# Second attention's score product moved between the halves of its query projection, and two small vector steps reordered

## The reference, cut to what matters

```python
x = _layernorm(x + _L0_attn_ref(x, qkv_weights))
# second attention
qh = _xpos(x @ Wq);  kh = _xpos(ctx @ Wk, inverse_scale=True);  vh = ctx @ Wv
scores = jnp.einsum('bld,bmd->blm', qh, kh) * decay_mask
x = _layernorm(x + scores @ vh)
x = _layernorm(x + _L0_ffn_ref(x, ...))        # shared expert, 2 of 8 routed experts
```

## Time and profile before

| what | value |
|---|---|
| median of 3 runs | 727.16 us (726.34 to 728.71) |
| profiled execution, its own time | 723.76 us |
| its span | 721.7 us |
| TensorE busy | 683.2 us, 95% |
| VectorE busy | 489.2 us, 68% |
| ScalarE busy | 478.9 us, 66% |
| GpSimd busy | 343.1 us, 48% |
| mean granted TensorE clock | 0.990 of full speed |

### The profile page before, as it was taken

One profiled execution on the slowest core, in us unless ns is written; L12 is line 12 of the kernel. 1 busy time (PEld: TensorE's weight loads), 2 busy tenths in 40 slices (PEclk: granted clock), 3 DMA queues, 4 the chain that ended last, 5 costly groups with the idle time before them and its releaser, 6 DMA issues.

```text
span 721.7 us, 21540 instructions
## 1 busy us (share of the span) xinstructions
PE 683.2 (95%) x6174; PEld 588.5 (82%) x6175; DVE 489.2 (68%) x1563; ACT 478.9 (66%) x1319; POOL 343.1 (48%) x469
## 2 busy tenths in 40 slices
PE   7989999999999999999998899889999999999994
PEld 5868888888888888888887555779999999998653
DVE  3666878888888888888896376445555555554266
ACT  0367888888888888888884242356666666666256
POOL 1001323435645455454455355055665556556495
PEclk9999999999999999999999899999999999999998
DMA  8743367424523233232336024686777777777597
GB/s 306 236 146 114 116 204 240 137 88 147 158 88 96 67 91 105 86 107 83 104 97 198 31 89 143 198 221 126 140 134 139 133 139 136 135 137 130 124 349 261
DMA packets 93947, 104.30 MB, mean 145 GB/s; under 512 B 13200, under 2 KB 86672, under 8 KB 92976
## 3 DMA queue, kind: packets, MB, share of 16 engines
q1 hardware_dynamic: 78480, 79.43, 37.2%
q0 software_dynamic: 14688, 23.26, 16.4%
q10 hardware_dynamic: 704, 0.66, 0.3%
HBM read 62.21 MB, written 41.10 MB: 143 GB/s over the span
## 4 chain that ended last, share of the span: by engine, by line
PE 78%; DVE 5%; DMA 5%; POOL 4%; issue 4%; SPq 3%; ACT 1%; DVEq 0%; POOLq 0%; ACTq 0%
PE ps L1051 15%; PE ps L1060 8%; PE ps L806 6%; PE ps L908 5%; PE ps L794 5%; PE ps L816 4%; PE ps L771 4%; PE ps L739 4%; PE ps L911 4%; PE ps L774 4%; PE ps L932 4%; DMA xg<-sent 3%; POOL first_use L715 2%; PE ps L1038 2%; PE ps L826 2%
## 5 line engine op out<-in xcount | busy, mean ns | idle before, releaser
L1118 ACT ACTIVATE prob<-ps,nmax 128x128 f32<-128x128 f32 x512 | 147.0, 380 | 27.4 <-DVE nmax L1332 27.4
L1051 PEld LDWEIGHTS ps<-xgT,attn_only 128*128 128x128 f32 x1136 | 136.0, 192 | 7.4 <-DVE ghT L1614 2.2
L1051 PE MATMUL ps<-xgT,attn_only 128*128 128x128 f32 x1136 | 138.9, 275 | 1.1 <-ACT xgT L1230 1.1
L674 POOL DMA_INDIRECT total<-rot,result_row x71 | 111.6, 1572 | 36.8 <-issue 34.3
L1332 DVE TENSOR_REDUCE nmax<-ps 128x4 f32<-128x512 f32 x128 | 82.2, 685 | 17.7 <-PE ps L794 17.0
L1614 DVE SCALAR_TENSOR_TENSOR ghT<-ps,attn_only 128x128 f32<-128x128 f32 x142 | 43.3, 347 | 71.0 <-PE ps L1051 59.3
L615 POOL TENSOR_TENSOR rot<-products 128x128 f32<-128x128 f32 x128 | 61.3, 499 | 57.1 <-DVE products L1342 57.0
L1125 ACT COPY pT<-ps 128x512 f32<-128x512 f32 x124 | 74.4, 600 | 20.8 <-PE ps L806 16.4
L806 PE MATMUL ps<-tf,prob 128*128 128x128 f32 x512 | 77.9, 275 | 4.4 <-DVE pT L1447 3.3
L641 POOL DMA_INDIRECT sent<-packets,pos x64 | 63.6, 993 | 35.6 <-PE ps L794 20.9
L1060 PE MATMUL ps<-first_use,ghT 128*128 x284 | 74.9, 386 | 0.0
(11 more groups left out here) (143 smaller groups left out, 1408.1 us busy)
## 6 DMA issues: line engine op xcount, KB each, us to landing
xg<-sent SPq DMA_DIRECT2D x71, 130.5 KB, 2.1
attn_only<-in_L_ffn_rb SPq DMA_DIRECT2D x71, 130.0 KB
first_use<-total SPq DMA_DIRECT2D x12, 512.0 KB, 8.7
total<-zeros POOLq DMA_DIRECT2D x3, 1408.0 KB, 8.0
k_dram<-first_use SPq DMA_DIRECT2D x4, 1024.0 KB, 4.6
attn_only<-in_x_turned SPq DMA_DIRECT2D x32, 128.0 KB, 2.5
attn_only<-k_dram SPq DMA_DIRECT2D x256, 16.0 KB
attn_only<-in_x SPq DMA_DIRECT2D x32, 128.0 KB, 2.7
```

Source lines behind the costliest of these rows:

```text
L674: eng.indirect_dma_start(totals[slot % 2], bass.IndirectOffsetOnAxis(ap=result_row[:, slot:slot + 1], axis=0), yw[:, slot, :], None, compu ...
L1051: mm = eng.matmul(ps[:, 2 * r + half, f * P:(f + 1) * P], w_now[:, r, c, cols:cols + P], xgT[:, r, c, :], start=(c == 0), stop=(c == DC - 1))
L1118: ins = eng.activation(prob[:, t % 2, 4 * u + n, :], SCORE[u][:, n * P:(n + 1) * P], ACT.Exp, bias=nmax[:, t % 2, 4 * u + n:4 * u + n + 1])
```

## The change

TensorE's four matmuls of the second attention's queries (two halves of two) no longer stand together ahead of the scores: the first half comes first, then the scores of the batch before, then the second half, which raises `xq_made`. VectorE takes the decay (`scx`) ahead of the products of the queries. At the end of VectorE's step the addition of the constant to the second variance stands ahead of the last mask. No instruction is added or removed.

```diff
+            def cross_queries(t, m):
+                for c in range(DC):
+                    mm = eng.matmul(Q_TURNED[:, m, :], xwq_sb[:, c, m * P:(m + 1) * P], x1T[:, t % 2, c, :],
+                                    start=(c == 0), stop=(c == DC - 1))
+                return mm
+
+            def cross_scores(t, n):
+                eng.wait_ge(rot_k_set, 2 * t + 2)
+                eng.wait_ge(rot_q_set, 2 * t + 2)
+                if live(n - 3):
+                    eng.wait_ge(pk_set, 2 * (n - 3) + 2)
+                else:
+                    bank7_read(n)
+                for m in range(2):
+                    mm = eng.matmul(SCX, rot[:, t % 2, m, :], rot[:, t % 2, 2 + m, :], start=(m == 0), stop=(m == 1))
+                mm.then_inc(scx_made, 1)
...
-                    for m in range(2):
-                        for c in range(DC):
-                            mm = eng.matmul(Q_TURNED[:, m, :], xwq_sb[:, c, m * P:(m + 1) * P], x1T[:, t % 2, c, :],
-                                            start=(c == 0), stop=(c == DC - 1))
-                    mm.then_inc(xq_made, 1)
...
+                    cross_queries(t, 0)
+                if live(n - 4):
+                    cross_scores(n - 4, n)
+                if live(t):
+                    cross_queries(t, 1).then_inc(xq_made, 1)
                 shared_between(n)
...
-                if live(t3):
-                    turned(t3, 2, Q_TURNED, xq_made, pq_set, rot_q_set)
                 if live(t4):
                     eng.wait_ge(scx_made, t4 + 1)
                     eng.tensor_tensor(scx[:, r4, :], SCX, decay, ALU.mult).then_inc(scx_set, 1)
+                if live(t3):
+                    turned(t3, 2, Q_TURNED, xq_made, pq_set, rot_q_set)
...
                     aggregate(t4, bn2, mv2, bn2_set, mv2_set)
+                    add_eps(t4, mv2, mv2_set)
                 if live(n) and live(n + 1) and n > 0:
                     lay_mask(n + 1, 3)
-                if live(t4):
-                    add_eps(t4, mv2, mv2_set)
```

More of the change, by code:

```diff
@@ L929, in step @@
                         eng.wait_ge(res2_set, n - 4)
-                    for m in range(2):
-                        for c in range(DC):
-                            mm = eng.matmul(Q_TURNED[:, m, :], xwq_sb[:, c, m * P:(m + 1) * P], x1T[:, t % 2, c, :],
-                                            start=(c == 0), stop=(c == DC - 1))
-                    mm.then_inc(xq_made, 1)
-                t = n - 4
-                if live(t):
[L938 to L946, removed]
+                    cross_queries(t, 0)
+                if live(n - 4):
+                    cross_scores(n - 4, n)
+                if live(t):
+                    cross_queries(t, 1).then_inc(xq_made, 1)
                 shared_between(n)
```

## The result

The changed kernel took 742.15 us (741.09 to 744.67, six runs), against 727.41 (724.37 to 729.93, six runs) for the kernel before: 1.0196 times as long, with a 95% interval of 1.0166 to 1.0225. The forecast was 742.9. The profiled execution took 741.09, its span 739.1, against 723.76 and 721.7.

What follows compares the result with a forecast made beforehand. TensorE was taken as the bound, with one 0.39 us stop per step. 29 x 0.50 = 14.5, plus 0.44 (step 33) and 0.8 (step 34), together 15.7, on the median 727.16 gave 742.9 us; range 735 to 748.

Steps and rivals of the forecast that it cites:

- The scores' wait: TensorE: scores behind the first query half wait for the keys' products, start at 0.78; TensorE stands for 0.33 us.
- Restarting: TensorE after a stop: scores take 0.07 us more, the output product L973 0.10 more.
- What is late next: Queries' products on VectorE end at 2.69; the output product waits until 2.84, 0.40 us later than before.
- The path through `res2`: Second path to the next projection: first residual takes 0.41, `res2` ends at 3.99, seen at 4.13, inside the projection's 4.17.
- The rival with a blocked residual: GpSimd still blocks VectorE's first residual, which takes 0.70: 0.59 us per step, 745.5 us; chance 0.13.
- The third edit: Second variance's constant ahead of the last mask on VectorE: the mask's delay is covered, earlier rows win nothing: 0.
- Per step: Projection of the next batch starts at 4.17 against 3.67: 0.50 us more per step, 29 steps, 14.5 us.
- The last steps: Pipeline's end: step 33 costs 0.44 us; step 34, with TensorE at half clock, 0.8, between 0 and 0.86.
- The sum: Steps 4 to 32 with steps 33 and 34: together 15.7 us slower, 742.9 us on the median.
- Both waits covered: Rival: keys' products end by 0.29, so scores and output lose nothing; 728.4 to 731.3 us; chance 0.09.
- The stop simply goes: Rival: output does not wait for the queries' products; 28 to 29 stops of 0.39 go, about 716 to 717 us; faster 0.07.
- The clock: Rival: TensorE's extra stops bring one more half-clock stretch, about 3 us: 746 us; chance 0.05.

Runs made afterwards that it cites:

- Experiment 4: Changed kernel with the keys' products ahead of `rden` on VectorE; 741.86 us, ratio 1.0173 to the kernel before.
- experiment 3: Kernel before with only the scores moved between the query halves on TensorE, VectorE's order unchanged; 755.05 us, ratio 1.037.
- experiment 2: Kernel before with only the decay moved ahead of the queries' products on VectorE, TensorE's list unchanged; 734.83 us, ratio 1.0078.
- experiment 8: Changed kernel with three of four query matmuls ahead of the scores instead of two; 736.63 us, ratio 1.0125 to the kernel before.
- experiment 6: Kernel before with the transposed rows put into bank 5, so they no longer wait for the decay; 724.64 us, ratio 0.9966.
- experiment 1: Kernel before with only the second variance's constant added ahead of the last mask; 727.23 us, ratio 0.9981.
- experiment 5: Kernel before with the decay placed between the two products of the queries on VectorE; 725.21 us, ratio 0.9963.
- Experiment 7: As experiment 6, with GpSimd's additions of the queries' products also waiting for the decay; 724.21 us, ratio 0.995 to the kernel before.

## Why the prediction was right, step by step

- **The scores' wait.** Put at 0.78, measured 0.77. Experiment 4 moved the keys' end and with it everything behind; experiment 3 shows that the scores' move alone makes the wait. The sentence that nothing on VectorE can give the wait back was too strong: in experiment 4 the keys' products ahead of `rden` ended 0.08 earlier, and the step was 0.09 shorter.
- **Restarting.** The scores took 0.68 and L978 0.67 after their stops, against 0.61 and 0.60; I had 0.07 and 0.10 in the sum. The interval from L978 to the projection is 1.31, not 1.33, and this is the 0.02 by which the step was put too long.
- **What is late next.** The products were put at 1.93 to 2.69 and L978 at 2.84; measured 1.94 to 2.70, and 2.84. Experiments 2 and 8 change this wait from two sides, and the step follows within 0.01 of what was expected.
- **The path through `res2`.** The statistics ended by 3.49 and `res2` at 3.97, against 3.99 forecast; the projection at 4.15 stays just behind it. With 0.42 for the residual the cover held. The rival with a blocked residual didn't come about, because GpSimd starts 0.16 behind the residual here. The Trainium skill (SBUF — State Buffer, Who interferes with whom) would have the later of the two blocked until the other is through, which would make a blocked residual about 0.89 (an estimate); experiments 3 and 6 measured 0.70 in that order, as the kernel before did.
- **The third edit.** Costed at nothing; experiment 1 agrees, with an interval from -0.4% to nothing.
- **Per step.** 0.50 was forecast, 0.48 measured; 29 steps give 13.9 instead of 14.5.
- **The last steps.** Step 33 cost 0.45 (0.44). The one mis-sized term is step 34: the sum has 0.8 for a half of the queries at half clock, and the changed kernel's step 34 had the full clock. There the scores go 1.62 after the first query matmul and the shared expert's matmuls 2.59; in experiment 1, where the scores go 1.66 after it at full clock by then, these start 2.18 after it. So it cost about 0.4. The prediction took it that the half clock would come in step 34 again; it came around the start of that step in the profiles of all eight experiments, but not in this one.
- **The sum.** 13.9 + 0.45 + 0.41 is 14.8, and the medians are 14.7 apart. That they agree to 0.1 is partly luck: the interval reaches from 12.1 to 16.4, the last two terms are read from one profile, and it is the fastest of the changed kernel's six runs. What the rows carry is the 0.48 a step, 13.9 of the whole. The profiled spans are 17.4 apart, and the 2.6 beyond the sum are no part of the theory: stretches of both signs, the largest the wait for "remote", which experiments without the change have too.
- **The rivals.** "Both waits covered" would need the keys' products by 0.29; they end at 0.63. "The stop simply goes" fails at L978, and experiment 2, which removes only that stop, is slower. The clock stayed full through the steady part.

## What to carry to other kernels

A wait that ends last is not a cost that can be struck off: before moving its producer forward, look up what else was covered by the old order (here 0.89 of query records covered the keys' products) and what the producer is put ahead of (here the products, which the next instruction needed as well). Where two readers wait for one engine, splitting the longer producer and placing the shorter between its parts let both wait less (experiment 5), while either order as a whole served one. And an edit should be tried alone and with the others: here one edit costs 0.29 by itself and repairs 0.37 of what the other costs.

## What the runs showed of the hardware

- A VectorE addition of 256 columns, the first residual, takes 0.42 when it starts 0.16 ahead of GpSimd's additions, and 0.70 when it starts 0.04 behind them; experiments 3 and 6 agree with the kernel before. Experiment 7 moved only GpSimd's start, and the 0.70 became 0.42. So the order of two starts some 0.2 apart sets 0.28 us.
- After a stop a TensorE group of four records took 0.68 instead of 0.61, and one of two records of 256 columns 0.67 to 0.70 instead of 0.60. This is small beside the stops, but the steady steps of the changed kernel pay both.
- A stretch at half clock came ahead of step 34 in nine of the ten profiles, starting 3.0 to 5.5 us before its first query matmul, but its length was 3.4, 6.8 or 10.2 us, so that in some of them it covered that step's queries and in some it ended before them (404 to 410 us in the kernel before: 0.50; the same in experiment 1: 0.72). The changed kernel's profile had none from 380 to 430 (1.00). Experiment 1 had a second one at 380 to 384 (0.57), the kernel before had not. A step's price read at half clock in one execution need not hold in the next.
- VectorE's `place` waited for "remote" once in nine of the ten profiles, 5.1 us in the changed kernel and 5.7 to 6.4 in the experiments, and in the kernel before's not at all. What it is, is open; nothing was tried on it.
